# A two-layer decoder on one core: finer first steps, small work and normalizations on GpSimd, and three PSUM banks each for decays and for products

## What is computed

```python
# layer 0
x = norm(x + mamba(x))            # sequential state over 256 tokens, 512 channels x 16 states
x = norm(x + softmax(layernorm(x @ (kv kv^T) / 16)))      # kv = ctx @ W_k.T + b_k
x = norm(x + experts(x))          # 8 experts, width 176, top 2 of a softmax; shared part 352
# layer 1
x = norm(x + gated_recurrence(x))
x = norm(x + (1 - g) * x + g * A)  # A: top 76 of 256 scores of the context, made symmetric
x = norm(x + experts(x))          # 8 experts, width 128, top 2; shared part 256

def mamba_step(state, a, bu, c):  # a = exp(dts * A), bu = dts * B * hs
    state = a * state + bu        # 512 channels x 16 states
    return state, (state * c).sum(states)
# dts = softplus(...), hs = silu(conv of 4 taps)
```

## Time and profile before

| | before |
|---|---|
| median of 3 runs | 667.3 us (667.09 to 668.12) |
| the profiled execution | 664.68 us |
| its span in the profile | 662.9 us |
| PE busy | 543.9 us, 82% |
| DVE busy | 525.3 us, 79% |
| ACT busy | 427.4 us, 64% |
| POOL busy | 227.0 us, 34% |
| first and last start of a scan instruction (L1102) | 51.8 and 499.6 us |

### The profile page before, as it was taken

One profiled execution on the slowest core, in us unless ns is written; L12 is line 12 of the kernel. 1 busy time (PEld: TensorE's weight loads), 2 busy tenths in 40 slices (PEclk: granted clock), 3 DMA queues, 4 the chain that ended last, 5 costly groups with the idle time before them and its releaser, 6 DMA issues.

```text
span 662.9 us, 8987 instructions
## 1 busy us (share of the span) xinstructions
PE 543.9 (82%) x2504; PEld 390.2 (59%) x2504; DVE 525.3 (79%) x1261; ACT 427.4 (64%) x955; POOL 227.0 (34%) x333
## 2 busy tenths in 40 slices
PE   4938564689877965899779998998899999999957
PEld 3526353457755643577557766767577668677634
DVE  0248988897889998999899979999999896664342
ACT  2468753798976973994999688969994632262211
POOL 1023654524552554355254424644440101101000
PEclk9778657689959996899889999999999999999969
DMA  7194010256006601472006703620470233224000
GB/s 220 40 382 157 0 65 0 57 137 225 0 1 194 197 13 63 123 214 66 1 0 176 234 1 95 190 61 1 136 210 2 66 117 102 62 67 141 0 9 8
DMA packets 29297, 63.56 MB, mean 96 GB/s; under 512 B 4864, under 2 KB 8192, under 8 KB 28736
## 3 DMA queue, kind: packets, MB, share of 16 engines
q1 hardware_dynamic: 29248, 62.98, 30.9%
HBM read 61.85 MB, written 1.11 MB: 95 GB/s over the span
## 4 chain that ended last, share of the span: by engine, by line
PE 44%; DVE 34%; issue 13%; ACT 6%; DMA 1%; POOL 0%; DVEq 0%; SPq 0%; POOLq 0%; ACTq 0%
PE work L552 25%; PE work L603 8%; DVE acc L1118 6%; DVE st L1102 6%; PE h_bank L528 5%; PE work L528 4%; DVE m L1053 3%; DVE wk L1057 2%; DVE h_tok L1012 2%; DVE du L1029 2%; DVE bst L940 2%; ACT dA L888 2%; DVE row L948 1%; DMA skip<-in_skip 1%; DVE mv L941 1%
## 5 line engine op out<-in xcount | busy, mean ns | idle before, releaser
L498 POOL TENSOR_TENSOR dbu<-du,b_rows 128x512 f32<-128x512 f32 x128 | 162.6, 1271 | 125.5 <-DVE st L1102 95.0
L888 ACT ACTIVATE dA<-dts,a_neg 128x127 f32<-128x127 f32 x512 | 156.8, 355 | 29.9 <-DVE st L1102 28.9
L1102 DVE TENSOR_TENSOR_SCAN st<-dA,dbu 128x512 f32<-128x512 f32 x128 | 155.7, 1217 | 14.9 <-ACT dA L888 13.1
L528 PE MATMUL h_bank<-ident,st 128*128 128x128 f32 x512 | 90.2, 310 | 40.4 <-DVE st L1102 40.2
L552 PE MATMUL work<-stream,xsT 128*128 128x352 f32 x320 | 112.4, 491 | 5.5 <-DVE h_tok L1012 3.3
L528 PEld LDWEIGHTS h_bank<-ident,st 128*128 128x128 f32 x512 | 69.0, 160 | 71.6 <-DVE st L1102 57.8
L1118 DVE SCALAR_TENSOR_TENSOR acc<-h_bank,c_cols,acc 128x512 f32<-128x512 f32 x128 | 93.7, 732 | 14.2 <-PE h_bank L528 9.7
L552 PEld LDWEIGHTS work<-stream,xsT 128*128 128x128 f32 x320 | 60.2, 202 | 35.6 <-DVE h_tok L1012 5.7
L521 POOL TENSOR_TENSOR rstd<-var,mhalf 128x1 f32<-128x1 f32 x32 | 18.3, 572 | 121.8 <-DVE var L942 93.8
L764 ACT ACT_TABLE_LOAD x44 | 56.5, 1283 | 3.2 <-PE work L552 2.5
L1012 DVE SCALAR_TENSOR_TENSOR h_tok<-h_tok,wf,work 128x176 f32<-128x176 f32 (+2 forms) x136 | 43.6, 374 | 15.7 <-PE work L552 15.6
(11 more groups left out here) (155 smaller groups left out, 846.2 us busy)
## 6 DMA issues: line engine op xcount, KB each, us to landing
stream<-in_stream SPq DMA_DIRECT2D x80, 352.0 KB, 3.7
stream<-in_stream SPq DMA_DIRECT2D x32, 384.0 KB, 3.6
b_rows<-b_dram SPq DMA_DIRECT2D x32, 256.0 KB, 4.9
stream<-in_stream SPq DMA_DIRECT2D x8, 256.0 KB, 2.8
wg<-in_wg SPq DMA_DIRECT2D x1, 1280.0 KB, 8.0
wu<-in_wu SPq DMA_DIRECT2D x1, 1280.0 KB, 10.6
wd<-in_wd SPq DMA_DIRECT2D x1, 1280.0 KB, 13.3
xT<-in_xT SPq DMA_DIRECT2D x4, 256.0 KB, 4.0
```

Source lines behind the costliest of these rows:

```text
L498: gp.tensor_tensor(tile, du[:, batch % 2, :, lo:hi], b_rows[:, b % 2, k:k + 1, :].to_broadcast([P, ET, P]), ALU.mult).then_inc(s["dbu_read ...
L528: return nc.tensor.transpose(dst, src, ident[:, :])
L888: last = A(dA[i % DA_RING][:, t, 1:P], dts[:, batch % 2, t, lo + 1:hi], ACT.Exp, scale=a_neg[:, t, k:k + 1])
L1102: V.tensor_tensor_scan(st[:, i % ST_RING].rearrange("p t l -> p (t l)"), dA[i % DA_RING].rearrange("p t l -> p (t l)"), dbu[:, i % DBU_RIN ...
```

## The change

- **Rings.** `DA_RING` goes from 2 to 3 and `WORK` from 4 to 3: of the 8 PSUM banks three hold decays, three hold products, two turned states.
- **First steps.** Part 0 of the loads keeps only xT, the first half of `w_in`, `cw` and `cb`; `ident` and `skip` come in a later part, the second half of `w_in` and the context after them. `pre` has 7 steps where it had 5: hid0 and hid1 are steps of their own, PE makes dt before B, and Ln, `dts` and `du` are done in halves of 128 tokens, so that a unit waits for its half alone. ACT runs one Silu on a constant before all else. `a_log`'s Exp, the negation and the clearing of `dA` come earlier.
- **To GpSimd.** Variance plus eps (all normalizations but the one in `hgrn` 4), subtract and multiply (`normalize`, 48 instructions), `dts` and `du` of batches 1 to 3, and `a_first` (4 instructions where DVE had 16). DVE's steps that overwrite `r` now wait for POOL's row.
- **Experts by taking out.** In layer 0 the weight of each expert is the scores minus the scores from which MATCH_REPLACE8 has taken out the two largest; this replaces the index, the cast and the two comparisons.
- **Orders.** All four strings of `ORDER` and the string of `BANK` are new. On DVE the first 13 steps of adj of batch 0 now come before the first scan step, and the convolution of batch 1 after it. Between the first and the last scan step DVE has 43 steps of adj where it had 36, and 28 normalizations where it had 29. Of the work after the last turned state PE has 11 steps more (of `ffn0` of unit 5, `out` of unit 6 and `ffn1` of unit 3) and 3 fewer (adj).

The diff, cut to its core (of each order only the first line of two engines):

```diff
-DA_RING, DBU_RING, ST_RING = 2, 4, 4
+DA_RING, DBU_RING, ST_RING = 3, 4, 4
 ACC_RING = 4
 H_BANKS = 2
-WORK = 4
+WORK = 3
...
-PRE_STEPS, ADJ_STEPS = 5, ROUNDS + 5
+PRE_STEPS, ADJ_STEPS = 5 + LT, ROUNDS + 5
...
     "pe": [
-        "pp000asspppppaaaaaaaaaaaaapssppssppssssssssssssss000sss00000sssss00s00ss00s0s000s00000000s0sss000aa00s000spss0",
...
+        "ppp0aaaaaaaaaaaaaassppppp00ppsassssssssassaaaaaaaaaaaaasssssss0s00ssp0ssppp0000spsppssss0s0sss00sss00000s00s00",
...
     "dve": [
-        "saa00111pppppppppsasassaaspsssssssssssassa00ass0s00ss0s0s0s00ss00s0s00s000asaa000apppp000ss0000000asssaaas0s00",
...
+        "saa00111pppppaaaaaaaaaaappsasssssssspsssssssppppppssaaa00asss000ssss0s0s000sssss00s0spss00pppppps000s000ssss00",
...
-    ("pre", 0): ["hid0", "hid1"], ("pre", 2): ["bT", "dt", "cT"], ("pre", 3): ["z0", "z1"],
+    ("pre", 0): ["hid0"], ("pre", 1): ["hid1"], ("pre", 3): ["dt", "bT", "cT"], ("pre", 4): ["z0", "z1"],
...
-        w_in = load("w_in", [P, HT, 2 * E], d["w_in"], 0)
+        w_in = sb("w_in", [P, HT, 2 * E])
+        loads.append((w_in[:, :, 0:E], d["w_in"][:, :, 0:E], 0))
         cw = load("cw", [P, ET, KC], d["cw"], 0)
         cb = load("cb", [P, ET], d["cb"], 0)
-        ident = load("ident", [P, P], d["ident"], 0)
-        skip = load("skip", [P, ET], d["skip"], 0)
         w_x = load("w_x", [P, ET, TR + 2 * N], d["w_x"], 1)
         w_dt = load("w_dt", [P, E], d["w_dt"], 1)
         b_dt = load("b_dt", [P, ET], d["b_dt"], 1)
         a_log = load("a_log", [P, ET, N], d["a_log"], 1)
-        loads.append((ctxT[:, :, :], d["ctxT"].rearrange("c (b l) -> c b l", b=B), 2))
+        ident = load("ident", [P, P], d["ident"], 2)
+        skip = load("skip", [P, ET], d["skip"], 2)
+        loads.append((w_in[:, :, E:2 * E], d["w_in"][:, :, E:2 * E], 3))
+        loads.append((ctxT[:, :, :], d["ctxT"].rearrange("c (b l) -> c b l", b=B), 3))
...
+            def root_of(layer, variance, eps):
+
+                if eps:
+                    links[0] += 1
+                    gp.tensor_scalar(var[layer][:, :], variance, eps, None, ALU.add).then_inc(s["pool_link"], 1)
+                    pool.wait_ge(s["pool_link"], links[0])
+                    variance = var[layer][:, :]
+                gp.tensor_tensor(rstd[layer][:, :], variance, mhalf[:, :], ALU.pow).then_inc(rstd_ready[layer], 1)
+
+            gp.memset(ones[:], 1.0).then_inc(s["ones_ready"], 1)
...
+            gp.memset(top2[:], -1.0)
...
-            pool.wait_ge(loaded[0], part_size[0])
+            pool.wait_ge(loaded[2], part_size[2])
...
+            def normalize(key, i, u):
+                stage, k = key
+                layer = int(i > 3)
+                pool.wait_ge(*root(stage, k, u))
+                gp.tensor_scalar(rows(i, u), r[layer][:, :], mv[layer][:, 0:1], rstd[layer][:, 0:1], ALU.subtract,
+                                 ALU.mult).then_inc(row(i, u)[0], 1)
+
             for stage, b, k in pool_order:
+                if stage == "pre" and k >= 5 and b:
+                    u, p = LT * b + k - 5, b % 2
+                    lo, hi = (k - 5) * P, (k - 4) * P
+                    pool.wait_ge(s["sp_ready"], u + 1)
+                    gp.tensor_tensor(dts[:, p, :, lo:hi], dts[:, p, :, lo:hi], za[:, :, lo:hi], ALU.add)\
+                        .then_inc(s["dts_ready"], 1)
+                    pool.wait_ge(s["dts_ready"], u + 1)
+                    gp.tensor_tensor(du[:, p, :, lo:hi], dts[:, p, :, lo:hi], hs[:, p, :, lo:hi], ALU.mult)\
+                        .then_inc(s["du_ready"], 1)
...
-                        pool.wait_ge(s["du_ready"], batch + 1)
+                        pool.wait_ge(s["du_ready"], b + 1)
...
+                    if hands_on(b) and k == 1:
+                        pool.wait_ge(s["dts_ready"], LT * (batch + 1))
+                        if b == 0:
+                            pool.wait_ge(s["a_ready"], 1)
+                        else:
+
+                            pool.wait_ge(s["carry_ready"], hands.index(b) * N)
+                        gp.tensor_tensor(a_first[:, :, :], a_neg[:, :, :].rearrange("p t n -> p n t"),
+                                         dts[:, batch % 2, :, hi:hi + 1].rearrange("p t l -> p l t").to_broadcast([P, N, ET]), ALU.mult).then_inc(s["keep_exp"], 1)
...
-                    gp.tensor_tensor(rstd[0][:, :], var[0][:, :], mhalf[:, :], ALU.pow).then_inc(rstd_ready[0], 1)
+                    root_of(0, mv[0][:, 1:2], 1e-6 if (stage, k) == ("xat0", 1) else 1e-5)
+                    if (stage, k) != ("xat0", 1):
+                        i = {"out": 1, "xat0": 2, "ffn0": 3}[stage]
+                        if i == 3 and b >= 2:
+                            pool.wait_ge(*row(4, b - 2))
+                        normalize((stage, k), i, b)
...
+                        root_of(1, mv[1][:, 1:2], 1e-5)
+                        i = {("hgrn", 5): 4, ("hgrn", 6): 5}.get((stage, k), 6)
+                        if i == 6 and b:
+                            pool.wait_ge(s["out_done"], 16 * b)
+                        normalize((stage, k), i, b)
 
...
+            act.wait_ge(s["ones_ready"], 1)
+            A(es[:, :], ones[:, :], ACT.Silu)
...
-                    A(za[:, :, :], za[:, :, :], ACT.Ln, bias=1.0).then_inc(s["sp_ready"], 1)
+                if stage == "pre" and k >= 5:
+                    if k == 5:
+                        act.wait_ge(s["exp_ready"], b + 1)
+                    lo, hi = (k - 5) * P, (k - 4) * P
+                    A(za[:, :, lo:hi], za[:, :, lo:hi], ACT.Ln, bias=1.0).then_inc(s["sp_ready"], 1)
...
-                link(V.bn_aggr(mv[layer][:, :], bst[layer][:, :]))
-                V.tensor_scalar(var[layer][:, :], mv[layer][:, 1:2], eps, None, ALU.add).then_inc(var_ready[layer], 1)
-
-            def normalize(key, i, u):
-                stage, k = key
-                layer = int(i > 3)
-                dve.wait_ge(*root(stage, k, u))
-                V.tensor_scalar(rows(i, u), r[layer][:, :], mv[layer][:, 0:1], rstd[layer][:, 0:1], ALU.subtract,
...
+                V.bn_aggr(mv[layer][:, :], bst[layer][:, :]).then_inc(var_ready[layer], 1)
 
             def add_bank(n, u, rows_, layer=0):
+                if n == "mamba" and u:
+                    dve.wait_ge(*row(3, u - 1))
+                if n == F0.stage:
+                    dve.wait_ge(*row(2, u))
+                if n == F1.stage:
+                    dve.wait_ge(*row(5, u))
...
-                    link(V.max_index(out=i8[lay][:, :], in_max=t8[lay][:, :], in_values=sc[:, :]))
-                    route(0, t8[0])
+
+                    link(V.tensor_copy(top2[:, 0:2], t8[lay][:, 0:2]))
+                    link(V.match_replace(out=rest[:, :], in_to_replace=top2[:, :], in_values=sc[:, :], imm_value=0.0))
+                    link(V.tensor_tensor(wf[lay][:, 0:8], sc[:, :], rest[:, :], ALU.subtract))
...
+                if stage == "pre" and k == 2 and b == 0:
+                    for t in dA:
+                        last = V.memset(t[:, :, 0:1], 0.0)
+                    last.then_inc(s["dA_cleared"], 1)
+                    dve.wait_ge(s["a_exp"], 1)
+                    V.tensor_scalar(a_neg[:, :, :], a_neg[:, :, :], -1.0, None, ALU.mult)\
+                        .then_inc(s["a_ready"], 1)
+                if stage == "pre" and k >= 5 and b == 0:
+                    u, p = LT * b + k - 5, b % 2
+                    lo, hi = (k - 5) * P, (k - 4) * P
+                    dve.wait_ge(s["sp_ready"], u + 1)
+                    V.tensor_tensor(dts[:, p, :, lo:hi], dts[:, p, :, lo:hi], za[:, :, lo:hi], ALU.add)\
+                        .then_inc(s["dts_ready"], 1)
+                    dve.wait_ge(s["dts_ready"], u + 1)
+                    V.tensor_tensor(du[:, p, :, lo:hi], dts[:, p, :, lo:hi], hs[:, p, :, lo:hi], ALU.mult)\
+                        .then_inc(s["du_ready"], 1)
...
-                        if k == 0:
-                            dve.wait_ge(s["du_ready"], batch + 1)
-                        if b == 0 and k == 0:
-                            for t in dA:
-                                last = V.memset(t[:, :, 0:1], 0.0)
-                            last.then_inc(s["dA_cleared"], 1)
-                        if hands_on(b) and k == 0:
-                            if b:
-
-                                dve.wait_ge(s["carry_ready"], hands.index(b) * N)
-                            for t in range(ET):
-                                last = V.tensor_scalar(a_first[:, :, t], a_neg[:, t, :], dts[:, batch % 2, t, columns(b)[1]:columns(b)[1] + 1],
-                                                       None, ALU.mult)
-                            last.then_inc(s["keep_exp"], 1)
```

283 lines of the change are left out of this document (132 added, 151 removed).

## The result

The change makes the kernel slower: 689.4 us in the median of 4 runs (687.7 to 690.4) against 667.2 (666.8 to 668.1) for the kernel before on the same chip, ratio 1.033 [1.030, 1.035]. Forecast were 645 us and a range of 627 to 668. The profiled execution took 690.35 us, with a span of 688.3.

The account below looks back on a forecast made before the run. It took DVE to set the pace of the scans and PE that of the next stage. Start 43, scans 424 and the rest 173.4 made a span of 640.4 us, given as 645 us, range 627 to 668.

Parts of the forecast that it names:

- The early start: Up to the first scan: it starts at about 43 us instead of 51.8, gain 8.8, bounds 40 and 48.
- 28 rows at 0.48, the price of `who` at the same shape: GpSimd in the scans: each moved normalization row takes 0.48 us, 13.4 us of added work in all.
- POOL's rows far above 0.48 us: Sign that the forecast is wrong: normalization rows on GpSimd taking far longer than 0.48 us each.
- Uncovered, the moved work costs only latency: Scans: after `bn_aggr` a row on GpSimd comes only some 0.15 to 0.5 us later.
- The serial end: Last unit's end, 23.5 us: keeps its order; normalizations and small sums on GpSimd add 1.5 us in all.
- DVE sets the pace: Scans: DVE, 92% busy, limits the 449.0 us; 33.0 less work and 8 more idle time give 424.
- +9.8: After the scans: work deferred on PE adds 9.8 us to that stage's 162.1.
- `T4`, `D3`, `D4` of `ffn0` 5 (2.9): After the scans: these deferred steps of unit 5's `ffn0` cost PE 2.9 us there.
- GpSimd as the feeder: Rival: in-order GpSimd delays `dbu` and holds up scans; above 667 from 22 us on, 680 at 35; chance 0.10.
- Three banks: Rival: three product banks make PE wait, 39 us instead of 8 if half counts; mostly 655 to 668; chance 0.12.
- The rest is not real: Rival: early gain holds, but the scans shrink only by DVE work lost before 350 us, -22; 656 us; chance 0.13.
- The third decay bank: Better case: it takes the 13 us DVE waited for ACT, and PE idles less in the tail; 624 us; chance 0.10.

Follow-up runs that it names:

- b_norm_pool: The kernel before with only the 48 normalization rows moved to GpSimd, as subtract and mult; ratio 1.017 to the kernel before.
- a_tail_banks: The changed kernel with six banks instead of three for the 130 claims behind the last turned state; ratio 1.032 to the kernel before.
- d_rows_fast: The changed code in the orders and banks of before, rows on GpSimd as mult and mult (mean not taken off); ratio 0.990 to the kernel before.
- a_code_b_order: All the changed code in the orders of before, with two decay banks and four for products; ratio 1.014 to the kernel before, 676.5 us by it.
- b_norm_fast: The kernel before with only the 48 rows on GpSimd, as mult and mult (mean not taken off); ratio 0.990 to the kernel before.
- a_row_fast: The changed kernel with its GpSimd rows as mult and mult (mean not taken off), own orders and banks; ratio 1.009 to the kernel before.

## Why the prediction was wrong

**The early start: the number was right in part by luck.** 43.8 us against 43. Of the steps, `cb` lands first and PE starts 1.6 us earlier (2.2 forecast). But `hs` comes 0.7 us earlier and not 3.5 (19.80 against 20.50), adj starts at 25.7 and not at 22, and takes 14.5 us and not 17, so `dts` and `du` of a half are done at 41.6 (40.3 forecast). The errors partly cancel. And the 51.8 from which 8.8 us were to be gained belongs to an execution in which TensorE was granted 0.66 of its clock between 20 and 30 us. That stretch in `before`, `b_norm_pool` (whose first steps are those of before), the change, and `a_tail_banks` (whose first steps are those of the change):

```profile
20.00:30.00 10.00, 8.35 (x32) 5.34 (x31) 0.41 (x2) 2.98 (x6) 0.00 (x0) 0.66 0.01 2
20.00:30.00 10.00, 10.00 (x57) 8.12 (x58) 0.20 (x1) 5.14 (x12) 0.00 (x0) 1.00 0.30 96
20.00:30.00 10.00, 9.27 (x51) 6.98 (x52) 4.51 (x19) 6.85 (x13) 0.00 (x0) 1.00 0.01 3
20.00:30.00 10.00, 9.23 (x26) 5.93 (x26) 1.29 (x6) 6.29 (x9) 0.00 (x0) 0.55 0.00 0
```

Their first scans start at 51.8, 47.1, 43.8 and 47.0 us. Like with like, the change gains 3.3 us at the full clock and 4.8 at the lower one. It comes with the new order: the finer first steps in the orders of before start at 47.7 (`d_rows_fast`, clock 1.00 in that stretch) and 52.3 (`a_code_b_order`, 0.62), no earlier than the kernel before.

**First wrong step: "28 rows at 0.48, the price of `who` at the same shape".** Same shape, other operations: measured 1.27. Another row of the same trace pointed the other way: `skip_diag`, a mult by one scalar without a second operation, took 604 ns for only 128 columns:

```profile
L474 POOL TENSOR_SCALAR skip_diag<-ident,skip 128x128 f32<-128x128 f32 x4 | 2.3, 604 | 8.5 <-DMA skip<-in_skip 8.5
```

No bound above 0.48 was given for the row, though its pair of operations had no row on GpSimd. I had named "POOL's rows far above 0.48 us" as a sign of being wrong, and it was. A form whose price is not in the trace needs a bound from another form, and `dbu` at 1.27 was there for it. Shown by the table of rows and orders: 16 us.

What was mis-sized with it is the latency. "Uncovered, the moved work costs only latency" was right, and "0.15 to 0.5 us later" was the term: with a row longer by 0.79 it is 0.9 to 1.3. That the price acts by this latency and not by GpSimd's busy time is argued, since the dear form lengthens both; for it speaks that no scan waits for `dbu`. In the orders of before the stage behind the scans goes from 164.0 (`b_norm_fast`) to 172.5 (`b_norm_pool`). Of these 8.5 us PE idles 3.8 more and is busy 4.7 more for the same 660 matmuls, at a granted clock of 0.92 instead of 0.95. The wait is paid a second time in slower matmuls; the other two pairs, with the dear form and without, show it too (149.6 against 147.6 us, and 165.8 against 161.6). The serial end was priced at +1.5 for this; it should have been counted for all 20 rows behind the scans.

**Second wrong step: "DVE sets the pace" of the scans, 449.0 - 33.0 + 8 = 424.** Two things failed in it.

The sum over DVE's work gave 33.0 us; 21.7 left. Nearly all of the gap lies in two terms. Rows were priced at 0.714 and not at 0.391. `b_norm_pool` moves the same 29 rows alone, and DVE's busy time in the window falls by 13.0 us, 0.45 a row, 7.7 less than counted. Part of the excess did not go with the moved instruction: the four `r<-row,g,S` of the window rise from 484 to 1016 ns there, and in the change `r<-r,ri,row` takes 927 ns where it took 775. The experts by taking out were to save 4.2 us. The six instructions took 7.7 us and the four that replace them 7.2, for the copy of two values (`top`) takes 0.55 and the last subtraction 0.40.

The step from busy time to time was wrong, and by more. DVE's idle time in the window was to go from 34.9 to 42.9 us and went to 60.0. A busy share of 92% over 449 us is no proof of a limit: with 29 us of DVE taken out and everything else the same, the window shrank by 3 to 10. The window is the sum of many stretches, in each of which another engine or a wait ends last; the earlier trace rows showed two of them, with PE at 97% and 93%, and I used them only for PE's capacity. So of the 25 us forecast nothing came: 452.4 us lies within the 449.0 to 455.9 of the unchanged kernel. The cheap form would have brought something: 441.8 in `a_row_fast`, 10.6 less, at clocks of 0.89 and 0.86.

**Third: the work deferred behind the scans.** +9.8 was mis-sized, 14.0 measured at one clock. The largest miss is in "`T4`, `D3`, `D4` of `ffn0` 5 (2.9)": the whole down product of unit 5 runs behind the last scan, 28 matmuls and 6.8 us. What failed with it is the other side: deferring was to be paid by a window shorter by 25, and the window gave back 2.0. Together with the start (earlier by 2.8 against `d_rows_fast`) this leaves 10.9 us of span, 13 by the ratios.

**The account.** Behind the scans +30.0: PE busy +21.1, of it 14.0 for deferred work and the rest, 7.1, slower matmuls; PE idle 17.4 to 26.3, +8.9. With -8.0 at the start and +3.4 in the window it is +25.4, the difference of the two spans; by the medians it is 22.2. Some 3 to 5 of the 8.0 at the start are the clock of that one execution before, and the +3.4 is within what one window can be off. Against the forecast of 640.4 the span is 47.9 longer: 0.8 at the start, 28.4 in the scans (11.3 of DVE's work, 17.1 of its idle time), 18.7 behind them.

**The rivals.** GpSimd as the feeder did not happen: no wait of a scan for `dbu` stands in the trace, though POOL was busy 264 us in the window. GpSimd did make it slower, by a dear row in each chain; that its queue held up the scans, as the rival had it, does not show. Three banks are ruled out behind the scans; within them they were not told apart from the new orders. "The rest is not real" had the right idea of the scans and took 22 us off all the same. The third decay bank brought nothing visible: DVE's wait for decays rose from 13.1 to 18.7 us.

**What stays open.** Why the new orders hold PE busy 8 us longer for the same matmuls (551.0 us in `a_row_fast`, 543.0 in `d_rows_fast`, clocks 0.905 and 0.901), and why rows on DVE cost 39 us more than cheap rows in them, and 4 in the old ones. Of orders, banks and rings, which costs the 13 us.

## What to carry to other kernels

Price an instruction by its operations as well as its shape, above all on GpSimd, and when the pair has no row, bound it by the dearest neighbour. Before work is moved off the "full" engine, cut that work out and see whether the stage shortens; if 29 us less give 3 to 10, moving them can give no more than that, and what the move adds comes off it. Take more than one profile of the kernel before as the base: a forecast stage by stage inherits the clock of the one execution that it is read from. Then count what the move adds to the latency of each serial chain, and count it again for the clock.
